# Adding the expert results two tiles at a time, and in another order, at the end of a transformer pair

## The reference

```python
aff = sigmoid(x @ wa); topk_p, topk_i = top_k(aff, 2)     # 16 experts, two for each token
routed = sum over the two chosen experts of share * expert(x)
shared = sum over two shared experts of expert(x)
return x + shared + routed
# expert(x) = (gelu(x @ g + gb) * (x @ w1 + b1)) @ w2 + b2, hidden width 256
```

## Time and profile before

| | |
|---|---|
| median of 3 runs (lowest, highest) | 1183.41 us (1183.01, 1184.33) |
| the profiled execution | 1186.92 us |
| its span, first to last instruction | 1185.2 us |
| busy in the span: TensorE, VectorE, ScalarE, GpSimd | 90%, 76%, 59%, 52% |
| mean granted TensorE clock | 0.938 of full speed |

### The profile page before, as it was taken

One profiled execution on the slowest core, in us unless ns is written; L12 is line 12 of the kernel. 1 busy time (PEld: TensorE's weight loads), 2 busy tenths in 40 slices (PEclk: granted clock), 3 DMA queues, 4 the chain that ended last, 5 costly groups with the idle time before them and its releaser, 6 DMA issues. The chain is left out here.

```text
span 1185.2 us, 25170 instructions
## 1 busy us (share of the span) xinstructions
PE 1064.9 (90%) x9375; PEld 784.6 (66%) x9375; DVE 897.9 (76%) x1634; ACT 698.6 (59%) x1103; POOL 616.0 (52%) x629
## 2 busy tenths in 40 slices
PE   5999997689997999878999989798898899999995
PEld 4777776634433667546777766596674788888883
DVE  5589998989999897667888888598755455655538
ACT  4565772668788555457888876394353254554430
POOL 5444445636567323348788887403784255555510
PEclk8999998979999999969999999658999799999998
DMA  8584431068777223222222220384896477678878
GB/s 306 188 256 121 163 90 63 1 187 191 208 189 203 91 61 116 77 79 55 55 55 55 56 54 2 125 324 163 198 257 206 146 244 242 232 244 284 299 274 301
DMA packets 117185, 191.45 MB, mean 162 GB/s; under 512 B 51361, under 2 KB 53559, under 8 KB 116141
## 3 DMA queue, kind: packets, MB, share of 16 engines
q1 hardware_dynamic: 100732, 146.26, 39.8%
q0 software_dynamic: 8544, 24.68, 6.8%
q10 hardware_dynamic: 7792, 18.96, 5.2%
HBM read 128.49 MB, written 44.47 MB: 146 GB/s over the span
## 5 line engine op out<-in xcount | busy, mean ns | idle before, releaser
L470 PE MATMUL ps_y<-kv,toep 128*128 128x288 f32 x640 | 156.5, 407 | 3.5 <-PEq L173 2.0
L470 PEld LDWEIGHTS ps_y<-kv,toep 128*128 128x128 f32 x640 | 121.2, 190 | 38.3 <-DMA toep<-taps_padded 3.0
L1653 POOL TENSOR_TENSOR vw<-at_pf,kw 128x1024 bf16<-128x1024 f32 x64 | 136.5, 2133 | 2.7 <-ACT kw L1713 2.7
L164 POOL TENSOR_TENSOR kv<-kx 128x1024 f32<-128x1024 f32 x32 | 60.6, 1893 | 84.2 <-DVE outT L524 37.8
L2639 POOL DMA_INDIRECT expert_results<-e_yo,target x47 | 68.4, 1455 | 58.0 <-ACT e_yo L2686 58.0
L1709 ACT ACTIVATE at_pf<-ps_st 128x1024 f32<-128x1024 f32 x64 | 65.5, 1024 | 39.5 <-PE ps_st L1849 35.5
L1760 DVE TENSOR_REDUCE at_negmax<-ps_s 128x4 f32<-128x1024 f32 x64 | 78.4, 1225 | 2.8 <-PE ps_s L1810 0.9
L1129 PEld LDWEIGHTS ps_eg<-e_xT,e_w 128*128 128x128 bf16 x1128 | 69.0, 100 | 14.4 <-issue 2.1
L1082 PE MATMUL ps_fH<-w1T,f_qaT 128*128 128x512 bf16 x256 | 65.7, 402 | 13.1 <-ACT f_h L987 8.0
L1129 PE MATMUL ps_eg<-e_xT,e_w 128*128 128x128 bf16 x1128 | 73.1, 223 | 3.4 <-DVE e_xT L2747 3.4
L1129 PE MATMUL ps_eu<-e_xT,e_w 128*128 128x128 bf16 x1128 | 72.3, 222 | 0.0
(11 more groups left out here) (463 smaller groups left out, 3105.6 us busy)
## 6 DMA issues: line engine op xcount, KB each, us to landing
e_parts<-down_parts SPq DMA_DIRECT2D x47, 512.0 KB
w_raw<-in_L_ffn_w ACTq DMA_DIRECT2D x32, 512.0 KB, 4.2
toep<-taps_padded SPq DMA_DIRECT2D x32, 256.0 KB
f_draw<-in_L_ffn_rw SPq DMA_DIRECT2D x16, 512.0 KB, 4.3
down_parts<-f_dparts SPq DMA_DIRECT2D x16, 512.0 KB, 2.9
expert_weights<-expert_results SPq DMA_DIRECT2D x16, 512.0 KB, 10.3
x_res<-in_x SPq DMA_DIRECT2D x4, 1024.0 KB, 5.5
c_in<-in_ctx SPq DMA_DIRECT2D x4, 1024.0 KB
```

Source lines behind the costliest of these rows:

```text
L164: pool.tensor_tensor(pairs[:, :, :, 0:HD0], x[:, :, 0:HD0].unsqueeze(2).broadcast_to([P, ROWS_N, WIDE, HD0]), sliding_rows(x, 0, 1, WIDE), ...
L470: last = pe.matmul(y[:, l * B:(l + 1) * B, :, WIDE - 1:], toep[h % 2][:, (DC - 1 - l + m) * P:(DC - l + m) * P], kv[h % 2][:, m * B:(m + 1 ...
L1653: pool.tensor_tensor(pl[u % 4][:, :, :, :], pf[u % 2][:, :, :, :], ph[u % 4][:, :, :, :], ALU.subtract)\
```

## The change

Results are added a chunk at a time: each add covers two tiles (128x1024 f32), so 32 adds become 16. Seven chunks are stored with one transfer of 512 KB each; the last chunk's two tiles are stored singly. VectorE's order becomes: gate and low part (0,0), chunk results 0, gate and low part (0,1), results 1, gate (1,0), results 2, low part (1,0), results 3, add_shared(0), results 4, gate and low part (1,1), results 5, 6 and 7, add_shared(1). Results 7, the last chunk's, are added before its shared sums; add_shared(1) waits for `done` to reach 8, and SyncE's last two stores wait for `shared_added` to reach 3 and 4.

```diff
-        TILES = [c * ST + s for c in ORDER for s in range(ST)]
+        out_chunk = out.rearrange("b s d -> (b s) d").rearrange("(i t p) d -> i p t d", p=P, t=ST)
...
-            for n, t in enumerate(TILES):
+            for n, c in enumerate(ORDER[:-1]):
                 sp.wait_ge(done, n + 1)
+                sp.dma_start(out_chunk[c, :, :, :], x[:, c * ST:(c + 1) * ST, :]).then_inc(out_stored, 16)
+            for s in range(ST):
+                t = ORDER[-1] * ST + s
+                sp.wait_ge(shared_added, ST + s + 1)
                 sp.dma_start(out_dram[t * P:(t + 1) * P, :], x[:, t, :]).then_inc(out_stored, 16)
-            sp.wait_ge(out_stored, 16 * NT)
+            sp.wait_ge(out_stored, 16 * (CH - 1 + ST))
...
             def add_shared(i):
+                if i:
+                    dve.wait_ge(done, CH)
                 for s in range(ST):
...
             def add_results(n):
-                t, late_n = TILES[n], n - (NT - len(LATE) * ST)
-                if late_n >= 0:
-                    dve.wait_ge(shared_added, late_n + 1)
-                dve.wait_ge(got_loaded[t // ST], 32)
-                dve.tensor_tensor(x[:, t, :], x[:, t, :], got[:, t, 0, :], ALU.add).then_inc(first_added, 1)
+                tiles = slice(ORDER[n] * ST, (ORDER[n] + 1) * ST)
+                if n == CN:
+                    dve.wait_ge(shared_added, ST)
+                dve.wait_ge(got_loaded[ORDER[n]], 32)
+                dve.tensor_tensor(x[:, tiles, :], x[:, tiles, :], got[:, tiles, 0, :], ALU.add).then_inc(first_added, 1)
                 dve.wait_ge(first_added, n + 1)
-                dve.tensor_tensor(x[:, t, :], x[:, t, :], got[:, t, 1, :], ALU.add).then_inc(done, 1)
+                dve.tensor_tensor(x[:, tiles, :], x[:, tiles, :], got[:, tiles, 1, :], ALU.add).then_inc(done, 1)
 
             late_gate(0, 0)
             late_low_part(0, 0)
+            dve.wait_ge(mid_loaded, 16 * NT)
+            add_results(0)
             late_gate(0, 1)
             late_low_part(0, 1)
-            dve.wait_ge(mid_loaded, 16 * NT)
-            add_results(0)
             add_results(1)
             late_gate(1, 0)
-            for n in range(2, 5):
-                add_results(n)
+            add_results(2)
             late_low_part(1, 0)
+            add_results(3)
             add_shared(0)
-            add_results(5)
-            add_results(6)
+            add_results(4)
             late_gate(1, 1)
             late_low_part(1, 1)
-            for n in range(7, 12):
+            for n in range(5, CH):
                 add_results(n)
-            add_results(12)
-            add_results(13)
             add_shared(1)
-            add_results(14)
-            add_results(15)
```

## The result

In 20 runs of each, the changed kernel takes 1181.03 us in the median (1176.15 to 1185.48) and the kernel before 1184.28 us (1180.54 to 1190.88). The ratio is 0.9969, 95% interval 0.9955 to 0.9983: 0.31% faster, 3.7 us with an interval of 2.0 to 5.3. The forecast was 1180.1 us, 3.3 us less than before.

The account below looks back on a forecast made before the run. VectorE's backlog of adds bounds the end: one tile fewer (1.33), narrower chunks (1.30) and closed idle time (0.93), less some 0.1, give 3.44 us; less 0.1 for stores, 1183.41 becomes 1180.1 us, range 1179.2 to 1182.0.

Parts of the forecast that it names:

- What bounds the end: Last stage: VectorE's backlog of adds sets the end; TensorE is done at 1172.4, ten us before VectorE.
- Price of a wide add: VectorE's result adds: 1.216 us per 128x1024 add, 2.40 per two-tile chunk against 2.66, 0.26 saved per chunk.
- 512 is wide enough: Reading of the skill on VectorE adds: wide adds worth nothing, sum loses 1.3 us, time 1181.4.
- at 512 and at 1024 alike: VectorE adds: 0.15 us of fixed time in each, at both widths.
- The exposed load: Before add_results(0), VectorE idles 1148.25 to 1149.5 for chunk 0; 2.1 us idle before late_low_part(1,0) is the slack.
- The moved gate: late_gate(1,1) starts at 1168.53 instead of 1167.32, its 0.84 us idle gone; TensorE's last 12 matmuls move to about 1170.9.
- hidden even at half clock: TensorE's last 12 matmuls before add_shared(1): at half the clock 5.5 us, ending at 1176.4.
- The stores: SyncE's last two stores, issued at 1178.7 and 1179.35: last landing taken as 2.1 us, bounds 2.0 and 3.2.
- Rival (a): Last two stores find a queue and become the end: landing 3.2 us, gain 2.2, time 1181.2; chance 0.09.
- had them clear at 1173.5: DMA engines before the last stores: full to about 1172.4 before, ten 256 KB stores instead of nine, clear at some 1173.5.
- The sum: Whole last stage: VectorE ends 3.44 us earlier, less 0.1 for the stores: 3.3 us, 1183.41 to 1180.1.
- The range: Kernel time 1179.2 to 1182.0 us: down by run scatter and small errors, up to take in the rivals' effects.

Follow-up runs that it names:

- e1: Changed kernel, each chunk's results added tile by tile (four 128x512 adds instead of two 128x1024): stretch from late_gate(0,0) to the end 37.16 us.
- e5: Changed kernel, three pieces of VectorE's list moved into gaps around late_low_part(1,0) and late_gate(1,1): stretch from late_gate(0,0) to the end 34.48 us.
- e6: Changed kernel, all VectorE gaps filled with half chunks, results 3 whole before late_low_part(1,0): stretch from late_gate(0,0) to the end 33.80 us, again 33.75.
- e2: Changed kernel, first chunk's results put behind late_low_part(0,1) again instead of before late_gate(0,1): stretch from late_gate(0,0) to the end 35.82 us.
- e3: Changed kernel, add_shared(1) before the last chunk's results again, both last stores after the last wide add: stretch from late_gate(0,0) to the end 36.43 us.
- e7: Changed kernel, GpSimd adds chunk 7 with two wide adds and VectorE leaves it out: stretch from late_gate(0,0) to the end 36.40 us.
- e4: Changed kernel, chunk 0 loaded third instead of first while VectorE still adds it first: stretch from late_gate(0,0) to the end 40.09 us.

## Why the prediction was right

- **What bounds the end.** VectorE's backlog, as stated. The runs that changed VectorE's list moved its end as expected, within 0.4 us: e1 +1.29, e5 -2.77, e6 -3.91 (expected +1.3, -2.4, -3.8), e2 and e3 -0.02 (expected none). In e7 it moved by +0.59, which is the 3.0 us that its slower adds cost less the 2.4 taken away.
- **Price of a wide add.** 1.22 us (taken: L509's 1.216), 2.40 for a chunk: 1166.32 to 1172.36 with its 1.23 is three chunks in 7.27 us, the forecast 7.27. "512 is wide enough" fell with e1. The 0.15 us of fixed time is a line drawn through two widths, so "at 512 and at 1024 alike" was put in, not read; what the runs show is the saving.
- **The exposed load.** Forecast as 1.25 us of idle time from 1148.25 to 1149.5; measured 1.63, and in the other runs that kept this load first 0.66 to 1.42. It was absorbed, as stated, by the idle time in front of late_low_part(1,0): forecast 2.1, measured 1.82, the difference being the later load. e4 shows the same from the other side.
- **The moved gate.** The 0.84 us in front of late_gate(1,1) went. TensorE's wait in late_down(1) grew from 0.21 to 1.41 us, with nothing behind it that is late. That its last 12 matmuls would be hidden even at half clock was put to the test by e7, by accident. There they took 5.30 us, from 1160.45 to 1165.75, after 4.39 us of idle time, at a granted clock of 0.50:

```profile
1160.60:1164.60 4.00, 4.00 (x10) 1.32 (x9) 3.93 (x4) 0.00 (x0) 0.00 (x0) 0.50 0.61 232
```

  The first tile's add of add_shared(1) began at 1165.22 and the second's at 1165.8, and the pair still ran in 1.28 us: hidden, but with nothing to spare there, as the list ahead of it was a chunk shorter.
- **The stores.** Taken 2.1 us to landing, measured 2.1; the tail behind VectorE grew by 0.12 us for the 0.1 forecast. Rival (a) did not happen, but it was near: by stretch the changed kernel's DMA engines are still full up to 1170 us and at 0.80 up to 1172,

```profile
1168.00:1170.00 2.00, 1.22 (x6) 0.37 (x4) 1.97 (x3) 0.00 (x0) 0.00 (x0) 1.00 1.05 408
1170.00:1172.00 2.00, 0.00 (x0) 0.00 (x0) 2.00 (x2) 0.00 (x0) 0.00 (x0) 0.88 0.80 307
```

  and the forecast had them clear at 1173.5 in the time of the trace before, which is 1169.1 here, 4.4 us less: this step was off by 1 to 2 us. It cost nothing, as the last two stores were issued only from 1174.34 on. With VectorE 2.8 us earlier (e5) the queue shows, and the landings of 3.0 and 3.4 us in e5 and e6 bear out the 3.2 us that rival (a) was priced with.
- **The sum.** VectorE's end came 3.44 us earlier in the stretch, to the hundredth; the steps were rounded by up to 0.1 us, so a match that close is luck, while one to 0.1 us is not. With the stores it is 3.32, forecast 3.3. The median of the 20 runs moved by 3.25 us, the ratio says 3.7 (2.0 to 5.3). The 1180.1 us itself is 0.9 under the measured 1181.03, since the kernel before measured 1184.28 in 20 runs and 1183.41 in the three that the forecast started from.
- **The scatter was taken too small.** The range leant on three runs that lie within 1.3 us, but the 20 runs of the same kernel spread over 10.3 us (1180.54 to 1190.88) and those of the changed one over 9.3. The working of the difference held; that the absolute time fell into a range only 2.8 us wide was in part luck with the starting point. That 2.4 us can be told from no change is not so for three runs: 20 runs of each left an interval of 2.0 to 5.3 us.

## What to carry to other kernels

When an engine has a backlog at the end, look for the last wait that something else sets (here late_low_part(1,0)); work moved ahead of it counts only as far as it fits in front of that wait, and the rest of the gain is what leaves the list behind it. That is why the early first chunk is worth nothing here (e2) while one more tile ahead of the low part and two fixed costs less per chunk are worth 2.6 us together; most of the rest is the 0.84 us gap in front of the last gate, which the later list closes. And before filling the last gaps, add up the bytes: 12.6 MB at about 390 GB/s held the stretch at 33.8 us in the best order tried, with VectorE done at 29.4.

## What the runs showed that was not expected

No edit changes an instruction ahead of the loads of the expert results, and yet the 14 profiles reach late_gate(0,0) up to 13 us apart (1132.60 to 1145.98); within one kernel it is 7.4 us in two profiles of the kernel before and 6.2 in three of the changed one. The 36 to 39 us behind it repeat to 0.06 us. Two profiles compared by their spans alone would have credited this change with 7.7 us.

TensorE's granted clock fell in e4 behind an idle time of 2.21 us. By stretch, in that kernel:

```profile
1149.00:1151.00 2.00, 0.90 (x5) 0.20 (x2) 1.67 (x3) 0.30 (x1) 0.00 (x0) 1.00 1.04 385
1151.00:1153.00 2.00, 0.89 (x4) 0.44 (x5) 1.63 (x2) 1.06 (x3) 0.00 (x0) 0.92 1.05 382
1153.00:1155.00 2.00, 2.00 (x6) 0.61 (x5) 1.97 (x4) 0.00 (x0) 0.00 (x0) 0.50 1.05 388
```

It had stood idle from 1149.90 us on, then ran 12 matmuls in 4.45 us from 1152.12 on, part of them at the lower of its two levels (0.50 is 1.2 GHz), where 2.76 is usual. Behind the 1.41 us of the changed kernel the clock stayed at 1.00. In e4 the slow matmuls cost nothing that shows: VectorE, with no idle time in front of late_low_part(1,0), was later still.
